# Layer norms rescheduled in a software-pipelined attention kernel, with another inverse root

## The reference, cut to what matters

```python
def _ln(x, w, b):
    mu = jnp.mean(x, -1, keepdims=True)
    var = jnp.mean((x - mu) ** 2, -1, keepdims=True)
    return (x - mu) * jax.lax.rsqrt(var + EPS) * w + b
attn_in = _adaln(x, cond, ...)              # _ln(x) * (1 + g) + bt
x = _attn(attn_in, attn_in, sa_...) + x     # 16 heads of 64, rotary, softmax
cross_in = _adaln(x, cond, ...)
ctx_n = _ln(context, ca_lnc_w, ca_lnc_b)
x = _attn(cross_in, ctx_n, ca_...) + x
ffn_in = _adaln(x, cond, ...)
x = gelu(ffn_in @ ff_w1 + ff_b1) @ ff_w2 + ff_b2 + x
```

## Time and profile before

| | us |
|---|---|
| median of 3 runs (1235.53 to 1237.63) | 1236.64 |
| the profiled execution, its own time | 1234.53 |
| its span, first to last instruction | 1232.7 |
| mean granted TensorE clock | 0.976 |

### The profile page before, as it was taken

One profiled execution on the slowest core, in us unless ns is written; L12 is line 12 of the kernel. 1 busy time (PEld: TensorE's weight loads), 2 busy tenths in 40 slices (PEclk: granted clock), 3 DMA queues, 4 the chain that ended last, 5 costly groups with the idle time before them and its releaser, 6 DMA issues.

```text
span 1232.7 us, 19200 instructions
## 1 busy us (share of the span) xinstructions
PE 1136.2 (92%) x7144; PEld 792.3 (64%) x7144; DVE 901.8 (73%) x1128; ACT 662.2 (54%) x925; POOL 702.8 (57%) x538
## 2 busy tenths in 40 slices
PE   3479999988999999999999999999999999985998
PEld 3356666655666666666656666666666666653997
DVE  3467787677877777788878777787778778865543
ACT  3245655465555555566656555555555555764321
POOL 1367575565666666686767666666666666763000
PEclk9689999989999999999999999999999999997999
DMA  5112111121112111211012111211121111200001
GB/s 166 34 35 63 41 36 31 48 68 32 35 35 69 35 36 35 65 35 31 23 35 64 35 35 35 65 35 35 35 64 35 35 36 35 86 1 1 18 18 35
DMA packets 47260, 52.13 MB, mean 42 GB/s; under 512 B 10688, under 2 KB 30144, under 8 KB 46912
## 3 DMA queue, kind: packets, MB, share of 16 engines
q1 hardware_dynamic: 45280, 49.32, 15.3%
q10 hardware_dynamic: 1888, 1.59, 0.4%
HBM read 15.22 MB, written 2.10 MB: 14 GB/s over the span
## 4 chain that ended last, share of the span: by engine, by line
PE 79%; DVE 6%; ACT 5%; issue 4%; POOL 2%; DMA 2%; SPq 1%; ACTq 0%; POOLq 0%; DVEq 0%
PE ps L733 13%; PE ps L589 10%; PE ps L590 10%; PE ps L591 10%; PE ps L677 5%; PE ps L702 5%; PE ps L721 5%; PE ps L679 4%; PE ps L683 4%; PE ps L681 4%; PE ps L798 4%; PE ps L710 2%; PE ps L599 1%; DVE neg_max L899 1%; SPq L300 1%
## 5 line engine op out<-in xcount | busy, mean ns | idle before, releaser
L451 ACT ACTIVATE probs<-ps 128x1024 f32<-128x1024 f32 x256 | 262.6, 1027 | 197.0 <-PE ps L683 180.2
L899 DVE TENSOR_REDUCE neg_max<-ps 128x2 f32<-128x1024 f32 x256 | 298.2, 1220 | 47.2 <-PE ps L702 46.9
L352 POOL TENSOR_TENSOR acc<-acc,probs 128x1024 f32<-128x1024 f32 x128 | 305.4, 2386 | 16.6
L360 POOL TENSOR_TENSOR eo<-tmp 128x512 f32<-128x512 f32 x64 | 94.0, 1468 | 242.7 <-DVE tmp L925 241.5
L733 PE MATMUL ps<-probs,v 128*64 128x512 f32 x1024 | 230.7, 592 | 0.0
L347 POOL TENSOR_TENSOR acc<-probs 128x1024 f32<-128x1024 f32 x64 | 152.9, 2388 | 101.6 <-ACT probs L451 101.3
L733 PEld LDWEIGHTS ps<-probs,v 128*64 128x64 f32 x1024 | 73.7, 137 | 145.7 <-issue 145.7
L925 DVE TENSOR_TENSOR tmp<-ps,rope 128x1024 f32<-128x1024 f32 x128 | 150.9, 1213 | 15.6 <-PE ps L591 15.6
L589 PE MATMUL ps<-xn_hi,w_hi 128*128 128x512 f32 x256 | 108.8, 425 | 19.7 <-issue 10.1
L702 PE MATMUL ps<-hi 64*128 64x512 f32 x512 | 105.7, 402 | 15.2 <-ACT v L489 6.8
L677 PE MATMUL ps<-max_rows,pick 64*128 64x512 f32 x512 | 111.4, 425 | 6.6 <-ACT max_rows L477 5.5
(11 more groups left out here) (110 smaller groups left out, 2314.9 us busy)
## 6 DMA issues: line engine op xcount, KB each, us to landing
lo<-eo SPq DMA_DIRECT2D x512, 64.0 KB, 2.0
w_raw<-pack_dram SPq DMA_DIRECT2D x16, 192.0 KB, 3.3
x<-x_dram SPq DMA_DIRECT2D x4, 512.0 KB, 11.1
w_raw<-pack_dram SPq DMA_DIRECT2D x8, 256.0 KB, 3.5
w_raw<-w_dram SPq DMA_DIRECT2D x2, 1024.0 KB, 5.2
out<-x SPq DMA_DIRECT2D x4, 512.0 KB, 2.9
ctx_in<-ctx_dram SPq DMA_DIRECT2D x4, 384.0 KB, 3.9
w_raw<-pack_dram SPq DMA_DIRECT2D x16, 96.0 KB, 2.4
```

The costliest lines, as they stand in the source:

```text
L352: pool.tensor_tensor(acc[:, g % 2, :, :], acc[:, g % 2, :, :], probs[:, i, :, :], ALU.add).then_inc(added, 1)
L451: act.activation(probs[:, i, :, :], score_ps(i), ACT.Exp, scale=SCALE).then_inc(exped, 1)
L899: dve.tensor_reduce(neg_max[:, i, :, 0], peak_ps(i), AX.X, ALU.max, negate=True).then_inc(maxed, 1)
```

## The change

The schedule of the norms gets a table `norm_at`: period of the statistics, of the z rows, of the transposes, and whether the first parts are done at once. Norms 1 to 3 and 8 to 11 do all three in one odd period; context norms in three periods (5, 6, 7; 9, 10, 11; 13, 14, 15; 17, 18, 19, instead of 5/6, 7/8, 9/10, 11/12); norms 12 to 14 in 59/60/61, 61/62/63, 63/64/65. The low parts come in the period after, behind the maxima on DVE. On PE the transposes always stand behind `project(p+4)`; the banks of the two halves change places; the loop runs two periods longer. The inverse root leaves POOL: ACT makes a guess exp(-0.5 ln(var)) and DVE does one Newton step, with four instructions in all (norms 0 and 15 too). `invert_root` with its 14 instructions, L867, NEWTON and I32 are deleted; `for p in range(FIRST, PAIRS + 1)` becomes `PAIRS + 3` on PE, ACT, DVE and POOL. Before `norm_rows(0)` and `norm_rows(LAST)` ACT calls `guess_rstd`, and DVE `refine_rstd` in the place of `invert_root`.

```diff
@@ -123,7 +120,7 @@
         def ln_ps(n, r):
-            return ps[:, (7, 6 if n == LAST else 1)[r], :]
+            return ps[:, (6 if n == LAST else 1, 7)[r], :]
...
@@ -203,15 +201,23 @@
-        stats_in = {-3: 1, -1: 2, 1: 3, 5: 4, 7: 5, 9: 6, 11: 7}
+
+
+        norm_at = {n: (2 * n - 5, 2 * n - 5, 2 * n - 5, True) for n in range(1, NB)}
         for b in range(NB):
-            stats_in[QUADS - 5 + 2 * b] = norm_of(X, 1, b)
-            stats_in[2 * QUADS - 5 + 2 * b] = norm_of(X, 2, b)
-        del stats_in[2 * QUADS + 1]
-        turned_in = {p + 1: n for p, n in stats_in.items()}
-
-        STATS = 2 * TT + 2
-        STEPS = 4 * NEWTON + 2
+            norm_at[norm_of(C, 0, b)] = (5 + 4 * b, 6 + 4 * b, 7 + 4 * b, False)
+            p = QUADS - 5 + 2 * b
+            norm_at[norm_of(X, 1, b)] = (p, p, p, True)
+        norm_at[norm_of(X, 2, 0)] = (PAIRS - 5, PAIRS - 4, PAIRS - 3, False)
+        norm_at[norm_of(X, 2, 1)] = (PAIRS - 3, PAIRS - 2, PAIRS - 1, False)
+        norm_at[norm_of(X, 2, 2)] = (PAIRS - 1, PAIRS, PAIRS + 1, False)
+        stats_in = {at[0]: n for n, at in norm_at.items()}
+        rows_in_period = {at[1]: n for n, at in norm_at.items()}
+        turned_in = {at[2]: n for n, at in norm_at.items()}
+        low_in = {at[2] + 1: n for n, at in norm_at.items()}
+
+        STATS = 2 * TT + 1
+        STEPS = 4
         ADA_STEPS = 4 * KT
...
@@ -312,7 +299,7 @@
                     load_weights(w + 1)
-                n = turned_in.get(p)
+                n = rows_in_period.get(p)
                 if n is not None and order[n][0] == C and order[n][1] + 1 < NB:
...
@@ -372,19 +359,17 @@
                     add_probs(p, 2)
-                n = stats_in.get(p)
-                if n is not None:
-                    invert_root(pool, n)
                 if is_pair(p):
                     add_probs(p, 3)
                 if is_job(p + 4):
                     rotate(p + 4)
+                n = rows_in_period.get(p)
                 if n is not None and order[n][0] == X:
                     add_bias(n)
             pool.wait_ge(rows_in, 16)
             add_bias(0)
-            for p in range(FIRST, PAIRS + 1):
+            for p in range(FIRST, PAIRS + 3):
                 period(p)
...
@@ -399,6 +384,12 @@
             act.dma_start(bias_rows[:, :, :], rows_d.partition_broadcast(128)).then_inc(rows_in, 16)
+
+            def guess_rstd(n):
+                act.wait_ge(ln_step, STATS * (n + 1))
+                act.activation(rstd[:, :], var_eps[:, :], ACT.Ln).then_inc(ln_guess, 1)
+                act.wait_ge(ln_guess, 2 * n + 1)
+                act.activation(rstd[:, :], rstd[:, :], ACT.Exp, scale=-0.5).then_inc(ln_guess, 1)
...
@@ -509,21 +500,28 @@
                     high_qk(p + 2)
+                n = stats_in.get(p)
+                at_once = n is not None and norm_at[n][3]
+                if at_once:
+                    guess_rstd(n)
+                    norm_rows(n)
                 if is_pair(p - 1):
                     high_o(p - 1)
                 if is_pair(p):
                     keep_av(p)
-                n = turned_in.get(p)
-                if n is not None:
-                    norm(n, 0)
-                    norm(n, 1)
                 if is_pair(p + 1):
                     keep_max(p + 1)
-                if p in stats_in:
-                    norm_rows(stats_in[p])
-                if p % 2 == 1 and is_quad(u + 1):
-                    keep_v(u + 1, 0)
-                    keep_v(u + 1, 1)
+                if n is not None and not at_once:
+                    guess_rstd(n)
+                keeps_v = p % 2 == 1 and is_quad(u + 1)
+                for r in range(2):
+                    if p in turned_in:
+                        norm(turned_in[p], r)
+                    if keeps_v:
+                        keep_v(u + 1, r)
+                n = rows_in_period.get(p)
+                if n is not None and not norm_at[n][3]:
+                    norm_rows(n)
                 if p in split_in:
...
@@ -594,6 +594,9 @@
                     pe.wait_ge(ln_rows, TT * (n + 1))
+                    p = norm_at[n][2] if n in norm_at else -1
+                    if p > 0:
+                        pe.wait_ge(av_kept, min(p + 1, PAIRS))
                 out = ln_ps(n, r)
...
@@ -665,7 +668,7 @@
                     if g - 1 in turned_in:
-                        pe.wait_ge(ln_scaled, 2 * turned_in[g - 1] + 2)
+                        pe.wait_ge(ln_scaled, 2 * turned_in[g - 1] + 1)
                 if kt >= 2:
...
@@ -692,7 +695,7 @@
                     if i == 1 and p - 1 in turned_in:
-                        pe.wait_ge(ln_scaled, 2 * turned_in[p - 1] + 1)
+                        pe.wait_ge(ln_scaled, 2 * turned_in[p - 1] + 2)
                 else:
...
@@ -748,20 +751,15 @@
                     turn_max(p + 1)
+                if is_job(p + 4):
+                    project(p + 4)
                 n = turned_in.get(p)
                 if n is not None:
-                    if is_pair(p):
-                        pe.wait_ge(av_kept, p + 1)
                     norm(n, 0)
                     norm(n, 1)
-                out_first = n is not None and order[n][0] == X
-                if not out_first and is_job(p + 4):
-                    project(p + 4)
                 if p % 2 == 0 and is_quad(u - 1):
                     project_out(u - 1, 0)
                     project_out(u - 1, 1)
-                if out_first and is_job(p + 4):
-                    project(p + 4)
                 if p % 2 == 1 and is_quad(u + 1):
...
@@ -863,9 +861,19 @@
                 dve.tensor_scalar(var_eps[:, :], mean_var[:, :, 1], EPS, None, ALU.add).then_inc(ln_step, 1)
-                dve.wait_ge(ln_step, STATS * n + 2 * TT + 1)
-                dve.tensor_scalar(rstd[:, :].bitcast(I32), var_eps[:, :].bitcast(I32), -0.5, RSQRT_GUESS,
-                                  ALU.mult, ALU.add).then_inc(ln_step, 1)
+
+            def refine_rstd(n):
+                dve.wait_ge(ln_guess, 2 * n + 2)
+                dve.tensor_tensor(newton[:, :], rstd[:, :], rstd[:, :], ALU.mult).then_inc(ln_newton, 1)
+                dve.wait_ge(ln_newton, STEPS * n + 1)
+                dve.scalar_tensor_tensor(newton[:, :], newton[:, :], -0.5, var_eps[:, :], ALU.mult, ALU.mult)\
+                   .then_inc(ln_newton, 1)
+                dve.wait_ge(ln_newton, STEPS * n + 2)
+                dve.scalar_tensor_tensor(rstd[:, :], newton[:, :], 1.5, rstd[:, :], ALU.add, ALU.mult)\
+                   .then_inc(ln_newton, 1)
+                dve.wait_ge(ln_newton, STEPS * n + 3)
+                dve.scalar_tensor_tensor(centre[:, :], mean_var[:, :, 0], -1.0, rstd[:, :], ALU.mult, ALU.mult)\
+                   .then_inc(ln_newton, 1)
...
@@ -947,31 +955,30 @@
                         peak(p + 1, i)
-                stats_now = p in stats_in
-                if stats_now:
-                    norm_stats(stats_in[p])
+                if p in low_in:
+                    norm_split(low_in[p], 0)
+                    norm_split(low_in[p], 1)
+                n = stats_in.get(p)
+                at_once = n is not None and norm_at[n][3]
+                if n is not None:
+                    norm_stats(n)
+                if at_once:
+                    refine_rstd(n)
                 if is_pair(p - 1):
                     normalise(p - 1)
                     low_o(p - 1)
-                if not stats_now and is_pair(p + 2):
+                if n is None and is_pair(p + 2):
                     low_qk(p + 2)
-                n = turned_in.get(p)
-                out_first = False
-                if n is not None:
-                    norm_split(n, 0)
-                    norm_split(n, 1)
-                    out_first = order[n][0] == X
-                if not out_first and is_job(p + 4):
+                if is_job(p + 4):
                     rotate(p + 4, 0)
                     rotate(p + 4, 1)
-                if stats_now and is_pair(p + 2):
+                if n is not None and is_pair(p + 2):
                     low_qk(p + 2)
+                if n is not None and not at_once:
+                    refine_rstd(n)
                 if p % 2 == 0 and is_quad(u - 1):
                     add_out(u - 1, 0)
                     add_out(u - 1, 1)
-                if out_first and is_job(p + 4):
-                    rotate(p + 4, 0)
-                    rotate(p + 4, 1)
                 if p in split_in:
```

More of the change, by code:

```diff
@@ L6 @@
 F32R = mybir.dt.float32r
-I32 = mybir.dt.int32
 ALU = mybir.AluOpType
@@ L24 @@
 EPS = 1e-5
-NEWTON = 3
-RSQRT_GUESS = float(0x5F3759DF)
 QKV = 3 * 128
@@ L147, in build @@
         ln_step = sem("ln_step")
+        ln_guess = sem("ln_guess")
         ln_newton = sem("ln_newton")
@@ L238, in loads_until @@
             return 16 * sum(LOADS[i // (NP // 2)] for i in range(w + 1))
[L240 to L257, removed]
         block = stack.enter_context(nc.Block())
@@ L540, in _ @@
             split_weights(0, 1)
```

(6 more changed lines are left out.)

## The result

Before, 1236.64 us; after, 1249.58 us (median of 5 runs, 1245.44 to 1252.85). The ratio of the two is 1.0105, 95% interval 1.0074 to 1.0136: slower by about 1%. The profiled execution took 1249.58 too, with a span of 1247.8, so spans may be compared as they stand: 15.1 us more than the earlier trace rows. The forecast was 15.2 more in the span and 1252 in the median.

The account below looks back on a forecast made before the run. TensorE bounds periods without a norm; only norm periods, start and end can change. Start -3.5, context +1.8, second sublayer +9.3 and end +7.6 give +15.2: 1249.7 for the profiled execution, median 1252 us, range 1239 to 1268.

Parts of the forecast that it names:

- The lock at four elements: On DVE: a four-element instruction with two tensor inputs waits for the rest of a POOL add, 2.4 us.
- The at-once norm: Norms 3, 8 to 11, done in one period: PE stalls 2.3 us for av, transposes add 1.0, period 18.8.
- The low parts of a context norm: Even context periods: subtractions behind the peaks meet POOL's adds, o_lo ends at 15.6, PE stalls 3.1 us.
- the context stage: Periods 6 to 21: 25.95 us over 15.5 each, against 24.1 before, so +1.8.
- the second sublayer: Periods 27 to 35: 165.4 us against 156.1 before, so +9.3.
- its own sign of being wrong: Norm stages: a granted clock below 1.00 there was listed among the signs that the forecast was wrong.
- Rival (b): PE: eight to fourteen stalls drop the clock and slow later matmuls, +20 to +35, 1272 to 1287 us; chance 0.08.
- Start: Start-up: norm 1 scaled in its own period, period 4 starts at 142.5 instead of 146.0, so -3.5 us.
- End: Period 60 onward: periods 60 to 62 take 51.3 against 45.5, +5.8; what follows +1.8; together +7.6 us.
- Rival (a): Refine and low parts are not held by POOL's adds: 1198 us, with half the collisions 1225; chance 0.2.
- Rival (c): ACT loads function tables for the guesses, 1.28 us each, two per at-once chain: +18, about 1270 us; chance 0.02.
- Rival (d): No change overall, because DVE's lateness is absorbed where the forecast counts it twice: 1234 to 1239 us; chance 0.06.

Follow-up runs that it names:

- the version that avoids most of them: Kernel after, with POOL waiting for low parts and refinement, context norms' guess behind the query split and refine behind o_lo: 1197.35 us, ratio 0.9699.
- both waits: Kernel after, with POOL waiting for the low parts before its second add and for the refinement before its third: 1209.94 us, ratio 0.9799.

## Why the prediction was right, and where it was not

The direction and the size came out: 15.1 for 15.2. The direction rests on a mechanism that the experiments show; that the sum agrees to 0.1 us is luck, since a cost left out and waits overstated cancel. Point by point:

- **The lock at four elements** (the bound between 0 and the rest of an add): right. 2.00 and 2.23 were measured where 0.16 is the free duration; the second refine instruction too takes its turn, at a mean of 0.60 between the start-up and the end. The two runs with POOL held show it by taking the meeting away.
- **The at-once norm:** the stall was 2.13, 1.6, 2.1 and 2.2 for a forecast of 2.3. Right in mechanism and size, but the period was 20.20 and not 18.8.
- **The low parts of a context norm:** 2.5 of stall for 3.1. POOL was ahead of VectorE as foreseen, by 0.07 us, but the pair of subtractions was through at 11.7 into the period, not 12.2. The periods were 19.8, not 18.55.
- **Both differences have one cause, the step that failed: pricing the matmuls behind a stall at full clock, everywhere but in periods 0 and 62.** 13.2 of the 15.1 us are the same 7144 matmuls running longer, 1.9 are waits. The forecast had no clock in its terms for the context stage and the second sublayer; there the matmuls took 3.5 and 8.5 more, and a granted clock below 1.00 in the norm stages, its own sign of being wrong, was seen (0.97 and 0.94). Rival (b) had this mechanism at a chance of 0.08 and on top of the waits; it came instead of a part of them. The argument against it was the clock of 1.00 in periods 60 to 62 in spite of 4.7 us of waiting; that total is in several pieces, the longest 2.3, and a period that kept its clock behind such a wait proves little, as periods 8 and 16 with POOL held for the refinement show. They and the run with dummy matmuls show the price, 1.5 us behind a wait of 2.5.
- **The waits were overstated,** which hid this. The context stage was to wait 1.8 more and waited 3.8 less: periods 13 and 21, put at 17.15 for a weight split between the rotate steps, were 15.48 and 15.52, and periods 10, 14 and 18, at 17.15 to 17.3, were 16.07 to 16.64. Periods 13 and 21 are a lateness counted twice: where periods 12 and 20 no longer stall (POOL held for the low parts), 13 and 21 do take 17.17 and 17.14, with a wait of 1.0 for neg_max. In the second sublayer 9.3 more were expected and 5.7 came. Period 28 was 18.23 and not 20.0, period 30 16.61 and not 17.25. Only the clock (+8.5) brought the stage to +14.2.
- **Start** 5.1 us gained for 3.5: norm 1 within its period did bring forward project(2), to 51.3 (49.6 forecast); period 0 begins at 72.3 (72.9 forecast). **End:** periods 60 to 62 took 51.33 for 51.3, with a wait of PE of 5.2 for o_lo in one piece; what follows them lasted 0.4 longer for 1.8 forecast.
- **Rival (a)**, small instructions slipping through, did not occur, but its sums were good: it had -12.5, -16.5, -6 and -4 for start, context, second sublayer and end without the meetings, 1198 in all, and the version that avoids most of them, which has other edits too, shows -13.7, -16.1, -4.5 and -3.4 in its spans, and 1197.35. **Rival (c):** the guess takes 0.21 for each of its two instructions, and its releases come 0.51 after var_eps; there is no room in it for a table load of 1.28. The Trainium skill, ScalarE: Activation LUTs, section "Table sets: the hidden batching unit", puts both functions in one set; the trace agrees, with two table loads in the whole kernel, as before. **Rival (d)**, a wash, did not come, but its mechanism, a lateness of VectorE counted twice, is part of why the waits were overstated, as in periods 13 and 21.

## What to carry to other kernels

When two engines exclude each other, ask for every small instruction on the critical one what the other has just started, whatever its own size: a wait in the engine with time to spare, placed by hand, was worth more here than making the small work smaller (30 and 21 us, for two and three lines). Forecast a period with a stall of TensorE of some 2 us twice, with the matmuls behind it at the full and at the lower clock (18.29 and 19.78 us for the same stall here), and check a forecast by its parts, PE busy and PE waiting apart, since a right total can be two wrong ones. Before counting work removed from an engine, look at the pause behind it; and before counting a stall removed, ask what it had been covering in the periods after.

## What the runs showed that was not expected

- A wait of PE of 1.9 to 2.5 us is often followed by 3 us of matmuls at about half their rate (256 columns every 0.21 instead of 0.12), and the window's clock reads 0.91 or 0.92. Not always: period 29 waited 1.6 for av, and period 32 of the kernel before 1.9 for av and 0.8 for xn_lo, both at 1.00. Period 14 waited the same 3.53 us for neg_max in three kernels and took 19.33 at 1.00 (POOL held for the low parts), 20.95 at 0.92 (both waits) and 21.80 at 0.84 (dummy matmuls). What decides it was not tried.
- An order of arrival decided by 0.07 or 0.13 us is worth 2.3 us to VectorE and up to 5.7 to the period. Edits elsewhere move the instructions into each other's way: period 14 took 15.97 to 16.07 in two of the kernels and 19.33 to 21.80 in four, none of which touched it, but all four of which had shortened period 12. A gain measured on such a kernel should be read by period, or it will be credited to the wrong edit.
